# Seven products per tile: ScalarE seeds PSUM banks for TensorE in place of sums on VectorE

## Chip, cores and metric

The kernel runs on one core of one Trainium2 chip. The metric is device time in microseconds; three runs of the kernel before gave 684.82, 685.51 and 687.89, median 685.51.

## The reference

A mixer block and a feed-forward block, each between a layer norm and a residual, on x of 4 x 512 x 512 in fp32, H = 2048:

```python
i, f, g = x @ Wi.T, x @ Wf.T, x @ Wg.T      # x layer-normed
gate = sigmoid(f); v = silu(i) * (1 - gate)
o = scan(gate, v)                            # along the 512 rows
o = rmsnorm(o) * gnorm_w * silu(g) @ Wo.T
x = x + layernorm(o)
h = silu(z @ W1.T) * (z @ W3.T)              # z = layernorm(x), 2048 wide
out = x + layernorm(fwht(h) @ W2.T)          # fwht: Walsh-Hadamard, folded into W2
```

## The kernel before

Each fp32 product is made of three fp16 passes (high x high, high x low, low x high, lines 611 to 613, `three_passes`), each a matmul with 128 rows of weights; weights and inputs are split into a high and a low half beforehand. The four batches b = 0 to 3 go through the same steps, overlapped. Every engine (PE is TensorE, ACT ScalarE, DVE VectorE, POOL GpSimd, SP the queue of the transfers) works through its own table of steps written out by hand at the top of the file (`PE_ORDER`, `ACT_ORDER`, ...), strictly in that order, and the engines meet through semaphores only. A step is named kind.b.index, on PE with the PSUM bank behind the colon. PE's kinds:

- XT: transposes of x; AN, GC, WS, W2S: norms of the weights; F, I, G: the three projections, each 12 matmuls of 512 columns; MS: mean square of o; Y: product with Wo; H2: Hadamard of W2.
- GA, UP (batch 0 only): product of z with a 128-wide chunk of W1 and W3.
- GP, GQ, GR, GU (batches 1 to 3, 16 groups g each): the same for two chunks at once by Strassen-Winograd's seven products. Group g = 2j is W1 for the pair of chunks 2j and 2j+1, g = 2j+1 is W3. A product is 2 x 3 matmuls of 256 columns. GP is P1 (line 796), GQ is P2 and P6 (805), GR P7 and P5 (808), GU P4 and P3 (811), through `two_products` (787); each kind has a bank of its own, and none waits for the result of another, only for its bank to be free and for the loaded weights (`ld_wc`).
- D: product of 128 rows of a hidden chunk with W2, 3 matmuls of 512 columns, 64 per batch, summed in banks 0 to 3; D.b.at is chunk at // 4.

The sums of the seven products are made outside PE. ScalarE's step GP copies P1 to SBUF (`copy_product`, line 986). VectorE's `combine_u2` (line 1282) adds it to P2 and to P6, 512 columns in one add; `combine_u3` (1292, 1295) adds U2 to P7 and P5 and makes one more sum of 256; `combine_last` (1303) adds P4 and P3. ScalarE's GA (line 1007) applies SiLU, VectorE's UP (1346) multiplies by the W3 part, ScalarE's UP (1019) makes the high half and POOL's UP (1434) the low half, after which D may read the chunk. ScalarE's UP also waits for `d_mm`, the D steps that still read its buffer.

PE's wait for a bank is derived from the table: a step waits for whoever read the bank's last contents (`wait_bank`). In VectorE's MS (line 1162) the mean square is read from its bank. The transfers that matter are `load_combined` (line 578, weights of a pair j, three slots), which waits for the products of the pair three back.

Of the kernel before, what the change touches and what calls it, by code (L numbers as in the profile page):

```python
# [1477 lines left out]
```

## Time and profile before

| | |
|---|---|
| median of three runs | 685.51 us (684.82 to 687.89) |
| profiled execution, span of its instructions | 683.7 us |
| PE, PE weight loads | 665.8, 403.8 us busy |
| DVE, ACT, POOL | 479.8, 292.7, 261.6 us busy |
| HBM | 81.92 MB read, 23.07 MB written |

The profile gives the profiled execution by its span, from first to last instruction; what lies around the instructions is in the device time and not in the span. Busy times say how long an engine worked; the idle time of an engine matters only where another one waits for it.

### The profile page before, as it was taken

What the parts mean: (1) busy time and instruction counts of PE and PEld (TensorE: products, weight loads), DVE (VectorE), ACT (ScalarE), POOL (GpSimd) and SP (SyncE); (2) the same over time, 40 slices, a digit from 0 to 9 for tenths busy, and PEclk for the clock granted to TensorE, in tenths of its full rate; (3) what the DMA queues carried; (4) which work ended last, traced back from release to release, by engine and by line L of the source; (5) the groups of instructions that cost most, each with busy time, mean ns of one, the idle gap of its engine ahead of it and who ended that gap; (6) DMA issues with size and microseconds to landing.
All of it is one profiled execution on the core that took longest, in us unless ns stands there. A gap on an engine that the chain in (4) does not pass through costs nothing.

```text
span 683.7 us, 10835 instructions
## 1 busy us (share of the span) xinstructions
PE 665.8 (97%) x4068; PEld 403.8 (59%) x4068; DVE 479.8 (70%) x836; ACT 292.7 (43%) x482; POOL 261.6 (38%) x228
## 2 busy tenths in 40 slices
PE   3999999999999999999999999999999999999996
PEld 2344454444444454567777785657567777777762
DVE  6998889988999878857577463456576555752554
ACT  4898974675245217623232312344234222321231
POOL 1189689558356200534422300233346211111231
PEclk9999999999999999999999999999999999999999
DMA  8961311413789985638496362202526846144122
GB/s 334 393 246 70 135 47 47 139 61 109 236 325 257 233 252 195 227 147 283 143 253 237 108 169 108 108 32 93 199 95 186 184 170 220 36 157 173 57 72 92
DMA packets 58819, 113.29 MB, mean 166 GB/s; under 512 B 33424, under 2 KB 37776, under 8 KB 54160
## 3 DMA queue, kind: packets, MB, share of 16 engines
q1 hardware_dynamic: 58768, 112.61, 49.7%
q8 instruction: 32, 0.52, 0.3%
q14 instruction: 19, 0.16, 0.1%
HBM read 81.92 MB, written 23.07 MB: 154 GB/s over the span
## 4 chain that ended last, share of the span: by engine, by line
PE 93%; DMA 3%; POOL 1%; SPq 1%; DVE 1%; issue 0%; ACT 0%; POOLq 0%; DVEq 0%
PE ps L611 30%; PE ps L613 30%; PE ps L612 30%; PE ps L759 2%; DMA w2t<-W2t 2%; DMA ring<-L_attn_Wf 1%; SPq L518 1%; PE ps L661 1%; POOL w2t L1420 1%; PE ps L720 0%; POOL rstd L1377 0%; POOL x1r L1420 0%; SPq L483 0%; ACT ot L861 0%; PE ps L683 0%
## 5 line engine op out<-in xcount | busy, mean ns | idle before, releaser
L611 PE MATMUL ps<-xb,ring 128*128 128x256 f16 (+1 forms) x704 | 226.0, 321 | 0.4 <-DVE ring L1105 0.4
L613 PE MATMUL ps<-xb,ring 128*128 128x256 f16 (+1 forms) x704 | 225.9, 321 | 0.0
L612 PE MATMUL ps<-xb,ring 128*128 128x256 f16 (+1 forms) x704 | 225.9, 321 | 0.0
L612 PEld LDWEIGHTS ps<-xb,ring 128*128 128x128 f16 x704 | 68.9, 98 | 48.1 <-issue 2.9
L611 PEld LDWEIGHTS ps<-xb,ring 128*128 128x128 f16 x704 | 69.1, 98 | 47.8 <-issue 2.6
L1377 POOL TENSOR_TENSOR rstd<-var,neg_half 128x1 f32<-128x1 f32 x64 | 45.3, 712 | 128.5 <-DVE var L1355 42.6
L613 PEld LDWEIGHTS ps<-xb,ring 128*128 128x128 f16 x704 | 68.9, 98 | 42.1
L1434 POOL TENSOR_TENSOR ring<-sga,ring 128x512 f16<-128x512 f32 x36 | 44.1, 1231 | 106.7 <-ACT ring L1019 106.7
L611 PE MATMUL ps<-ring 128*128 128x256 f16 x288 | 78.5, 273 | 0.0
L613 PE MATMUL ps<-ring 128*128 128x256 f16 x288 | 78.5, 273 | 0.0
L612 PE MATMUL ps<-ring 128*128 128x256 f16 x288 | 78.5, 273 | 0.0
L1434 POOL TENSOR_TENSOR hsp<-sga,hsp 128x512 f16<-128x512 f32 x24 | 28.3, 1190 | 96.6 <-ACT hsp L1019 96.6
L1282 DVE TENSOR_TENSOR ring<-ps,junk 128x512 f32<-128x512 f32 x48 | 33.0, 688 | 41.8 <-PE ps L613 28.5
L1292 DVE TENSOR_TENSOR ring<-ps,ring 128x512 f32<-128x512 f32 x48 | 33.0, 687 | 37.2 <-PE ps L613 36.3
L986 ACT ACTIVATE junk<-ps 128x256 f32<-128x256 f32 x48 | 18.2, 379 | 88.0 <-PE ps L613 84.9
L1303 DVE TENSOR_TENSOR ring<-ps,ring 128x512 f32<-128x512 f32 x48 | 33.0, 687 | 30.9 <-PE ps L613 30.6
L611 PE MATMUL ps<-w2t,ring 128*128 128x512 f16 x144 | 54.6, 379 | 0.0
L612 PE MATMUL ps<-w2t,ring 128*128 128x512 f16 x144 | 54.6, 379 | 0.0
L613 PE MATMUL ps<-w2t,ring 128*128 128x512 f16 x144 | 54.6, 379 | 0.0
L1346 DVE SCALAR_TENSOR_TENSOR sga<-ring,up_c,sga 128x512 f32<-128x512 f32 x48 | 37.1, 784 | 17.1 <-ACT sga L1007 16.1
L1007 ACT ACTIVATE sga<-ring,gate_c 128x512 f32<-128x512 f32 x48 | 34.0, 717 | 34.7 <-POOL hsp L1434 12.1
L1019 ACT ACTIVATE ring<-sga 128x512 f16<-128x512 f32 x36 | 22.2, 624 | 43.4 <-DVE sga L1346 28.2
(174 smaller groups left out, 1193.6 us busy)
## 6 DMA issues: line engine op xcount, KB each, us to landing
ring<-w_comb SPq DMA_DIRECT2D x24, 1792.0 KB, 7.6
ring<-W13t SPq DMA_DIRECT2D x16, 512.0 KB, 7.3
ring<-W13t SPq DMA_DIRECT2D x8, 1024.0 KB, 6.1
w_comb<-ring SPq DMA_DIRECT2D x8, 1024.0 KB, 8.1
rows<-L_attn_hidden_states SPq DMA_DIRECT2D x16, 256.0 KB, 4.6
w2t<-W2t SPq DMA_DIRECT2D x8, 512.0 KB, 10.2
res<-L_attn_hidden_states SPq DMA_DIRECT2D x16, 256.0 KB, 4.5
w_comb<-ring SPq DMA_DIRECT2D x8, 512.0 KB, 2.7
```

The lines of the kernel that those rows point to most:

```text
L611: pe.matmul(dst, a_hi, b_hi, start=start, stop=False)
L612: pe.matmul(dst, a_hi, b_lo, start=False, stop=False)
L613: return pe.matmul(dst, a_lo, b_hi, start=False, stop=stop)
L986: act.activation(p_copy[:, g % 2], bank("GP", b, g)[:, 256:512], ACT.Copy).then_inc(sp_rdy, 1)
L1007: act.activation(sga[:, c % 2], src, ACT.Silu, scale=gate_c[:]).then_inc(sga_rdy, 1)
L1019: act.activation(hid(b, c, 0), sga[:, c % 2], ACT.Copy).then_inc(hid_hi, 1)
L1282: dve.tensor_tensor(combined(g % 2)[:, 0:512].rearrange("p (o t) -> p o t", o=2), bank("GQ", b, g)[:].rearrange("p (o t) -> p o t", o=2), ...
L1292: dve.tensor_tensor(to[:, 512:1024].rearrange("p (o t) -> p o t", o=2), bank("GR", b, g)[:].rearrange("p (o t) -> p o t", o=2), both, ALU. ...
L1303: dve.tensor_tensor(to[:, 512:1024], bank("GU", b, g)[:], to[:, 512:1024], ALU.add).then_inc(gu_rdy, 1)
L1346: dve.scalar_tensor_tensor(sga[:, c % 2], src, up_c[:], sga[:, c % 2], ALU.mult, ALU.mult).then_inc(hid_rdy, 1)
L1377: pool.tensor_tensor(dst, src, neg_half[:].broadcast_to(src.shape), ALU.pow).then_inc(done, 1)
L1434: pool.tensor_tensor(hid(b, c, 1), sga[:, c % 2], hid(b, c, 0), ALU.subtract).then_inc(hid_lo, 1)
```

## The change

The seven products are ordered so that PE does part of the sums itself: a matmul series that doesn't start a bank anew adds to what is in it. GP now makes P1 and P5 in one bank. ScalarE copies P1 into both halves of the GQ bank (`seed_p1`) and P5 to SBUF. PE adds P2 and P6 onto the seed, which gives C11 and U2. ScalarE copies U2 over P1 (`seed_u2`). GR adds P7 onto U2 in the GQ bank and P3 onto the copy of U2 in the GP bank. VectorE adds P5 to each (`sum_c22`, `sum_c12`, 256 columns each), and GU adds P4 onto the half of the GQ bank that `sum_c22` has read. The GQ bank then holds two of the four quarters, which GA and UP for odd chunks read directly; even chunks read the sums in SBUF. GR and GU have no banks of their own. Three VectorE steps per group become two, one ScalarE step becomes two with three copies. All five order tables are new, in the part before the products too: POOL takes X1.1.2 and X1.1.3 ahead of the first butterflies FW, and PE takes F.0.0 ahead of AN.2.

```diff
@@ PE_ORDER (and the tables of ACT, DVE, POOL and SP, all written anew)
-GP.3.6:7 GQ.3.4:5 GR.3.4:6 D.3.0 GQ.3.5:4 GR.3.5:5 D.3.1 GP.3.7:7 GQ.3.6:6 D.3.2 GU.3.4:4 D.3.3
+D.2.63 GQ.3.4:4 D.3.0 GR.3.4 GQ.3.5:5 GP.3.6:7 GU.3.4 D.3.1 GR.3.5 D.3.2 D.3.3 D.3.4 D.3.5 D.3.6 GQ.3.6:4 GP.3.7:6
...
-        p_copy = junk[:].bitcast(F32).rearrange("p (w t) -> p w t", w=2)
-        def combined(w):
-            return kb(46 + 4 * w, 4).bitcast(F32)
+        p5 = junk[:].bitcast(F32).rearrange("p (w t) -> p w t", w=2)
+        def summed(g):
+            return kb(46 + 2 * (g % 4), 2).bitcast(F32)
...
-            at = c % 2 * 2 + t // 2
-            return hid(b, c - c % 2 + (0, 1, 1, 0)[at], part)[:, chunk((0, 2, 0, 2)[at] + t % 2)]
+            return hid(b, c - c % 2 + 1 - t // 2, part)[:, chunk(2 * (c % 2) + t % 2)]
...
+            elif k == "GP":
+                engine.wait_ge(c12_rdy, HC * (n - 1) + u + 1)
+            elif k == "GQ":
+                engine.wait_ge(hid_rdy if u % 2 else sga_rdy, HC * n + 2 * (u // 2) + 2)
...
-            def products_p1(b, g):
+            def products_p1_p5(b, g):
...
+                wait_bank("GP", b, g)
+                dst = bank("GP", b, g)
+                product(dst[:, 0:256], b, g, 0, 0, True, False, False)
+                product(dst[:, 256:512], b, g, 3, 3, False, True, False).then_inc(gp_mm, 1)
             def products_p2_p6(b, g):
-                two_products("GQ", b, g, (1, 1), (4, 4), gq_mm)
-            def products_p7_p5(b, g):
-                two_products("GR", b, g, (5, 5), (3, 3), gr_mm)
-            def products_p4_p3(b, g):
-                wait = up_mm if g % 2 else ga_mm
-                two_products("GU", b, g, (2, 6), (6, 2), wait, 2)
+                n = HC * (b - 1) + g
+                pe.wait_ge(seed_rdy, n + 1)
+                dst = bank("GQ", b, g)
+                product(dst[:, 0:256], b, g, 1, 1)
+                product(dst[:, 256:512], b, g, 4, 4).then_inc(gq_mm, 1)
+            def products_p7_p3(b, g):
+                n = HC * (b - 1) + g
+                pe.wait_ge(u2_rdy, n + 1)
+                product(bank("GQ", b, g)[:, 256:512], b, g, 5, 5).then_inc(gr_mm, 1)
+                pe.wait_ge(p5_rdy, n + 1)
+                product(bank("GP", b, g)[:, 0:256], b, g, 6, 2).then_inc(gr_mm, 1)
+            def product_p4(b, g):
+                n = HC * (b - 1) + g
+                pe.wait_ge(c22_rdy, n + 1)
+                product(bank("GQ", b, g)[:, 256:512], b, g, 2, 6).then_inc(up_mm if g % 2 else ga_mm, 2)
...
-            def copy_product(b, g):
+            def seed_p1(b, g):
                 n = HC * (b - 1) + g
                 act.wait_ge(gp_mm, n + 1)
+                wait_for_bank(act, "GQ", b, g)
+                src = bank("GP", b, g)
+                both = src[:, 0:256].rearrange("p (o t) -> p o t", o=1).broadcast_to((P, 2, 256))
+                act.activation(bank("GQ", b, g)[:].rearrange("p (o t) -> p o t", o=2), both, ACT.Copy).then_inc(seed_rdy, 1)
                 if n > 1:
-                    act.wait_ge(gq_rdy, n - 1)
-                act.activation(p_copy[:, g % 2], bank("GP", b, g)[:, 256:512], ACT.Copy).then_inc(sp_rdy, 1)
+                    act.wait_ge(c12_rdy, n - 1)
+                act.activation(p5[:, g % 2], src[:, 256:512], ACT.Copy).then_inc(p5_rdy, 1)
+            def seed_u2(b, g):
+                n = HC * (b - 1) + g
+                act.wait_ge(gq_mm, n + 1)
+                act.wait_ge(p5_rdy, n + 1)
+                act.activation(bank("GP", b, g)[:, 0:256], bank("GQ", b, g)[:, 256:512], ACT.Copy).then_inc(u2_rdy, 1)
...
-            def combine_u2(b, g):
-            def combine_u3(b, g):
-            def combine_last(b, g):
+            def sum_c22(b, g):
...
+                dve.wait_ge(p5_rdy, n + 1)
+                dve.wait_ge(gr_mm, 2 * n + 1)
...
+                dve.tensor_tensor(summed(g)[:, 256:512], bank("GQ", b, g)[:, 256:512], p5[:, g % 2], ALU.add).then_inc(c22_rdy, 1)
+            def sum_c12(b, g):
...
+                dve.wait_ge(gr_mm, 2 * n + 2)
+                dve.tensor_tensor(summed(g)[:, 0:256], bank("GP", b, g)[:, 0:256], p5[:, g % 2], ALU.add).then_inc(c12_rdy, 1)
```

How the tables move work, at three places. The first is PE in batch 3 at the end of GQ.3.7 (ps5 and ps6 are PSUM banks, `seed`, `u2`, `p5` and `c22` the semaphores of the steps named above; L643 to L645 are the three passes). Before, GR.3.7 follows GQ.3.7 directly in a bank of its own:

```order
L613 MATMUL ps5<-ring 128x256
L611 MATMUL ps4<-ring 128x256 [waits gu_rdy]
L612 MATMUL ps4<-ring 128x256
L613 MATMUL ps4<-ring 128x256
L611 MATMUL ps4<-ring 128x256
L612 MATMUL ps4<-ring 128x256
L613 MATMUL ps4<-ring 128x256
L611 MATMUL ps4<-xb,ring 128x256
```

And with the change, one step D stands between GQ.3.7 and GR.3.7:

```order
L645 MATMUL ps5<-ring 128x256
L643 MATMUL ps0<-w2t,ring 128x512 [waits hid_lo,hid_hi]
L644 MATMUL ps0<-w2t,ring 128x512
L645 MATMUL ps0<-w2t,ring 128x512
L643 MATMUL ps5<-ring 128x256 [waits u2_rdy]
L644 MATMUL ps5<-ring 128x256
L645 MATMUL ps5<-ring 128x256
L643 MATMUL ps5<-ring 128x256
L644 MATMUL ps5<-ring 128x256
L645 MATMUL ps5<-ring 128x256
L643 MATMUL ps6<-xb,ring 128x256 [waits p5_rdy]
```

GR now works in GQ's bank and waits for ScalarE's copy of U2, with D.3.12 in between; the wait before was for the bank alone.

The second is ScalarE in batch 1, between the hidden copies of chunks 10 and 12 (L1019, now L1029) and the products. Before:

```order
L1019 ACTIVATE ring<-sga 128x512 [waits d_mm,hid_rdy] x2
L986 ACTIVATE junk<-ps 128x256 [waits gq_rdy,gp_mm]
L1007 ACTIVATE sga<-ring,gate_c 128x512 [waits hid_lo,gr_rdy]
L1007 ACTIVATE sga<-ring,gate_c 128x512 [waits hid_lo,gu_rdy]
L1019 ACTIVATE hsp<-sga 128x512 [waits d_mm,hid_rdy]
L847 ACTIVATE o_s<-rows 128x512 [waits ld_zt,x_norm]
L1019 ACTIVATE hsp<-sga 128x512 [waits d_mm,hid_rdy]
L1007 ACTIVATE sga<-ring,gate_c 128x512 [waits hid_lo,gr_rdy]
```

With the change, UP.1.10 and UP.1.11 in the first row, then GA.1.12, GA.1.13, GP.1.14 (two copies), UP.1.12, UP.1.13 and GQ.1.14, the seed of U2, and GA.1.14:

```order
L1029 ACTIVATE ring<-sga 128x512 [waits d_mm,hid_rdy] x2
L1017 ACTIVATE sga<-ring,gate_c 128x512 [waits hid_lo,c12_rdy]
L1017 ACTIVATE sga<-ps,gate_c 128x512 [waits hid_lo,ga_mm]
L982 ACTIVATE ps<-ps 128x512 [waits sga_rdy,gp_mm]
L985 ACTIVATE junk<-ps 128x256 [waits c12_rdy]
L1029 ACTIVATE hsp<-sga 128x512 [waits d_mm,hid_rdy] x2
L991 ACTIVATE ps<-ps 128x256 [waits p5_rdy,gq_mm]
L1017 ACTIVATE sga<-ring,gate_c 128x512 [waits hid_lo,c12_rdy]
```

A seed that PE waits for (L991) stands right behind two hidden copies that wait for D; on PE the order there is D.1.39, GQ.1.14, D.1.40, GR.1.14.

The third is PE in batch 3 at MS.3.0, the mean square, followed by Y.3.0. Before, in banks 7 and 4:

```order
L613 MATMUL ps6<-xb,ring 128x256
L720 MATMUL ps7<-ones,osum 128x1 [waits oadd,gr_rdy]
L720 MATMUL ps7<-ones,osum 128x1 x3
L611 MATMUL ps4<-ring,ot 128x512 [waits gu_rdy,o_lo,o_hi]
L612 MATMUL ps4<-ring,ot 128x512
```

With the change both are in bank 6:

```order
L645 MATMUL ps5<-ring 128x256
L711 MATMUL ps6<-ones,osum 128x1 [waits oadd,c12_rdy]
L711 MATMUL ps6<-ones,osum 128x1 x3
L643 MATMUL ps6<-ring,ot 128x512 [waits e_rdy,o_lo,o_hi]
L644 MATMUL ps6<-ring,ot 128x512
```

Y.3.0 now waits for `e_rdy`, VectorE's read of the mean square.

## Rows read from the trace of the kernel before

**Rows 1.** Page: span, busy times, slices of PE and its granted clock
```profile
span 683.7 us, 10835 instructions
...
PE 665.8 (97%) x4068; PEld 403.8 (59%) x4068; DVE 479.8 (70%) x836; ACT 292.7 (43%) x482; POOL 261.6 (38%) x228
...
PE   3999999999999999999999999999999999999996
...
PEclk9999999999999999999999999999999999999999
```

**Rows 2.** Waits of PE, longest group: us, times, longest
```profile
PE ps L661 <- DVE rows L1075: 9.2, 3, 8.4
```

**Rows 3.** Chain that ended last, last matmul: start, us
```profile
672.55 0.23 PE ps L613
```

**Rows 4.** Timeline at 426.7 us: start, us, engine, line, operation
```profile
426.72 0.27 PE L613 MATMUL ps<-xb,ring 128*128 128x256 f16 x1
...
426.83 0.38 PE L611 MATMUL ps<-w2t,ring 128*128 128x512 f16 x1
...
427.03 0.39 ACT L986 ACTIVATE junk<-ps 128x256 f32<-128x256 f32 x1
...
427.05 0.38 PE L612 MATMUL ps<-w2t,ring 128*128 128x512 f16 x1
```

**Rows 5.** Groups by line and shape; the last row is line 850 alone
```profile
L612 PE MATMUL ps<-xb,ring 128*128 128x256 f16 x384 | 104.7, 273 | 0.0
...
L611 PE MATMUL ps<-ring 128*128 128x256 f16 x288 | 78.5, 273 | 0.0
...
L1434 POOL TENSOR_TENSOR ring<-sga,ring 128x512 f16<-128x512 f32 x36 | 44.1, 1231 | 106.7 <-ACT ring L1019 106.7
...
L1346 DVE SCALAR_TENSOR_TENSOR sga<-ring,up_c,sga 128x512 f32<-128x512 f32 x48 | 37.1, 784 | 17.1 <-ACT sga L1007 16.1
...
L1282 DVE TENSOR_TENSOR ring<-ps,junk 128x512 f32<-128x512 f32 x48 | 33.0, 688 | 41.8 <-PE ps L613 28.5 <-issue 6.5 <-ACT sga L1007 3.8
...
L1292 DVE TENSOR_TENSOR ring<-ps,ring 128x512 f32<-128x512 f32 x48 | 33.0, 687 | 37.2 <-PE ps L613 36.3
...
L1303 DVE TENSOR_TENSOR ring<-ps,ring 128x512 f32<-128x512 f32 x48 | 33.0, 687 | 30.9 <-PE ps L613 30.6
...
L1019 ACT ACTIVATE ring<-sga 128x512 f16<-128x512 f32 x36 | 22.2, 624 | 43.4 <-DVE sga L1346 28.2 <-PE ps L613 15.2
...
L1295 DVE TENSOR_TENSOR ring<-ps,ring 128x256 f32<-128x256 f32 x48 | 20.4, 424 | 1.6
...
L986 ACT ACTIVATE junk<-ps 128x256 f32<-128x256 f32 x48 | 18.2, 379 | 88.0 <-PE ps L613 84.9 <-DVE ring L1282 3.1
...
L850 ACT ACTIVATE xb<-ps x8: 572/584/598, 11.9 to 44.0; 128x512 f16<-128x512 f32 x8
```

**Rows 6.** Timeline: an engine's end and the weight load that waited for it
```profile
10.07 1.91 ACT L861 ACTIVATE ot<-ring 128x2048 bf16<-128x2048 f32 x1 [7.84 <-DMA ring<-L_attn_Wf]
...
12.03 0.13 PEld L683 LDWEIGHTS ps<-ot,ones 128*128 128x128 bf16 x2 [2.10 <-ACT ot L861]
...
24.27 1.41 DVE L1105 SCALAR_TENSOR_TENSOR ring<-ring,row_s 128x512 f16<-128x512 f32 x2
...
25.14 0.10 PEld L611 LDWEIGHTS ps<-xb,ring 128*128 128x128 f16 x1 [0.43 <-issue]
```

**Rows 7.** Timeline of PE: AN.2 and the first matmul of F.0.0
```profile
18.98 1.89 PE L683 MATMUL ps<-sga,ones 128*128 128x512 bf16 x4 [0.17 <-ACT sga L861]
...
20.66 0.42 PE L611 MATMUL ps<-xb,ring 128*128 128x512 f16 x1
```

**Rows 8.** Timeline: first matmul of Y.3.0, and VectorE's read for MS.3.0
```profile
484.24 0.38 PE L611 MATMUL ps<-ring,ot 128*128 128x512 f16 x1
...
484.41 0.16 DVE L1162 TENSOR_SCALAR ms_eps<-ps 128x4 f32<-128x4 f32 x1 [2.06 <-PE ps L720]
```

**Rows 9.** Page, DMA issues: count, KB each, us to landing
```profile
ring<-w_comb SPq DMA_DIRECT2D x24, 1792.0 KB, 7.6
```

More of the change, by code:

```diff
@@ L609, in _, with three_passes @@
         def _(pe):
[L610 to L613 removed]
+            def three_passes(dst, a_hi, a_lo, b_hi, b_lo, start, stop, onto=False):
+                pe.matmul(dst, a_hi, b_hi, start=start, stop=False, skip_group_check=onto)
+                pe.matmul(dst, a_hi, b_lo, start=False, stop=False, skip_group_check=onto)
+                return pe.matmul(dst, a_lo, b_hi, start=False, stop=stop, skip_group_check=onto)
@@ L659, in transpose_tile @@
+                wait_for_bank(pe, kind, b, t)
             def transpose_tile(dst, tile):
@@ L778, in up, with product @@
                 hidden("UP", b, c, 1, up_mm)
-            def product(dst, b, j, w, block, q, start, stop):
+            def product(dst, b, g, block, q, start=False, stop=True, onto=True):
+                j, w = divmod(g, 2)
                 for k in range(2):
@@ L783, in product @@
                     b_hi, b_lo = comb_z(b, q, 0)[:, k, :], comb_z(b, q, 1)[:, k, :]
-                    last = three_passes(dst, a_hi, a_lo, b_hi, b_lo, start and k == 0, stop and k == 1)
+                    last = three_passes(dst, a_hi, a_lo, b_hi, b_lo, start and k == 0, stop and k == 1, onto)
                 return last
-            def two_products(kind, b, g, one, two, done, by=1):
-                j, w = divmod(g, 2)
-                n = HC // 2 * (b - 1) + j
-                wait_bank(kind, b, g)
-                dst = bank(kind, b, g)
-                if one:
-                    product(dst[:, 0:256], b, j, w, *one, True, False)
-                product(dst[:, 256:512], b, j, w, *two, not one, True).then_inc(done, by)
-            def products_p1(b, g):
+            def products_p1_p5(b, g):
                 j, w = divmod(g, 2)
@@ L999, in ga @@
                 else:
-                    act.wait_ge(gu_rdy if c % 2 else gr_rdy, n - HC + 1 - c % 2)
-                    src = combined(0)[:, c % 2 * 512:c % 2 * 512 + 512]
+                    g = 2 * (c // 2)
+                    if c % 2:
+                        act.wait_ge(ga_mm, n + 1)
+                        src = bank("GQ", b, g)[:]
+                    else:
+                        act.wait_ge(c12_rdy, HC * (b - 1) + g + 1)
+                        src = summed(g)
                 if n == 0:
@@ L1343, in up @@
                 else:
-                    dve.wait_ge(gu_rdy if c % 2 else gr_rdy, n - HC + 2 - c % 2)
-                    src = combined(1)[:, c % 2 * 512:c % 2 * 512 + 512]
+                    g = 2 * (c // 2) + 1
+                    if c % 2:
+                        dve.wait_ge(up_mm, n + 1)
+                        src = bank("GQ", b, g)[:]
+                    else:
+                        dve.wait_ge(c12_rdy, HC * (b - 1) + g + 1)
+                        src = summed(g)
                 dve.scalar_tensor_tensor(sga[:, c % 2], src, up_c[:], sga[:, c % 2],
```

365 lines of the change are left out of this document (164 added, 201 removed).

## Prediction

> **What bounds the kernel now.** The page first: TensorE (PE) is busy for 665.8 of 683.7 us at the full granted clock, VectorE (DVE) for 70%, ScalarE (ACT) for 43%; of the 40 slices only the first and the last are below 9 [rows 1]. The waits of PE come next: the longest group is 9.2 us, 8.4 of it the start of the program, and the five groups together make 12.2 us, all before 25.2 us [rows 2]. From then to the last matmul at 672.55 us [rows 3] PE waits for nobody. That its busy time is real shows in the starts of single matmuls: 256 columns take 0.11 us to the next start, 512 take 0.22 [rows 4]. So the 647 us between are PE's own work, and a change can move the end in three ways only: change that work, change the 25 us ahead or the 11 us behind, or make PE wait where it doesn't today.
>
> **The work of PE.** Per product group (b, g) there are 7 products of 6 matmuls of 256 columns before and after; only their grouping changes, from 1+2+2+2 to 2+2+2+1. The trace has 3 x (384 + 288) = 2016 such matmuls [rows 5], which is 48 groups x 42. Cost: 0.
>
> **VectorE and ScalarE.** Removed per group on VectorE: 688 + 687 + 424 + 687 = 2486 ns; added: two adds of 256 columns, 2 x 424 = 848 ns [rows 5]. Over 48 groups VectorE loses 79 us of work (479.8 to about 401). ScalarE had one copy of 379 ns; it gets a seed of 512 columns, a copy of 256 to SBUF and a seed of 256. No row shows ScalarE writing PSUM; the nearest are its copies out of PSUM, 584 ns for 512 columns and 379 for 256 [rows 5]. I take these, so 1.34 in place of 0.38 us, +46 us in all (292.7 to about 339). Bounds: from 0.1 us less to 0.1 us more for each. Neither total is worth anything in itself, since PE waits for neither engine [rows 2]; both stay under 60%.
>
> **What is new: PE waits inside a group.** Before, no product needed another engine's answer; ScalarE and VectorE only had to free a bank. Now a group is a relay: P1, P5 on PE; seed on ScalarE; P2, P6; seed of U2 on ScalarE; P7, then P3; sum on VectorE; P4. One round trip costs: last matmul start to the start of the engine that waits, 0.31 us (426.72 to 427.03) [rows 4]; the operation; and the hand-over to PE, which is 0.05 us from ScalarE (10.07 + 1.91 to 12.03) and about 0.15 from VectorE (the first of two splits in the 1.41 us from 24.27, so an end near 25.0, to 25.14); I use 0.05 to 0.19 [rows 6]. What PE is given to do meanwhile I count from the two order tables: one step D is 3 x 0.216 = 0.65 us, one product of six 0.65; counted from the last matmul's start that is 0.65 + 0.11 = 0.76 us.
>
> - Seed of U2, the first place shown above: in 10 of 48 groups exactly one step of 0.65 us stands between (3.7, 2.6, 1.15 and so on). Needed: 0.31 + 0.38 + (0.05 to 0.19) = 0.74 to 0.88, there are 0.76. Wait 0 to 0.12, taken 0.06: 10 x 0.06 = 0.6 us. The other 38 have 1.3 us and more: 0.
> - Sum ahead of P4: in 10 groups only P3 stands between. Needed: 0.31 + 0.42 + (0.05 to 0.19) = 0.78 to 0.92 against 0.76. Wait 0.02 to 0.16, taken 0.09: 0.9 us.
> - First seed: one group (1.4) has one step, 0.76 us against 0.31 + 0.58 + (0.05 to 0.19) = 0.94 to 1.08: 0.3 us. The 47 others have at least 1.3 + 0.11: 0.
> - Step MS.3.0 and Y.3.0 now share bank 6, and Y.3.0 waits for VectorE's read. In the trace Y's first matmul starts at 484.24 and that read ends at 484.41 + 0.16 [rows 8]; with the hand-over 484.62 to 484.76: 0.4 us.
>
> On a round trip 0.1 us weighs 2 us over the twenty tight ones, so where the seed is written matters. The rows have PSUM to SBUF only. The Trainium skill (Perfetto Trace Analysis, Optimizing Scalar/DVE Operations) puts ScalarE's access overhead at about 93 ns on SBUF and 51 on PSUM; by that each U2 seed would be some 0.04 us shorter and the first term 0.2 in place of 0.6 us, an estimate from that page that no run here shows.
>
> **Queues.** ScalarE works in order, so a step that waits holds the seeds behind it. The tightest such place is the second shown above. UP.1.12 waits for the end of D.1.39 (its buffer is read until then). Call the issue end of D.1.39 zero: ScalarE starts at 0.2, two hidden copies of 0.626 take it to 1.45; GQ.1.14 ends on PE at 1.30, so its seed can start at 1.50 and is done at 1.88; PE wants GR.1.14 at 1.30 + 0.65 = 1.95. It fits, with 0.02 to spare after a hand-over of 0.05. Five more places (GP.2.2, GR.2.0, GQ.1.13, GQ.3.10, GQ.3.11) come out between 0.1 short and 0.3 spare; I take 0.2 us for all. The hidden values reach D later relative to it: least distance from the last product of a pair to the step D that reads it was 7.8 us, is now 4.55 (D.2.40), against 0.31 + 0.78 + 0.63 + 1.23 + hand-overs of 0.3 = 3.25 us [rows 5]; the sum of 0.69 that stood in it is gone. Cost 0, spare 1.3 us, or some 0.6 with one SiLU of about 0.7 queued ahead. If that cover went, each 0.1 us would show as a wait of D for GpSimd.
>
> **Transfers.** SP's and POOL's queues are reordered too. The weights of a pair are loaded when the pair three back is done; least distance in the order was 13.0 us, is 15.6, for 7.6 us to landing [rows 9]: 0. On POOL the first butterflies of W2 move behind two short powers; the first matmul on them comes after the attention part of batch 0: 0.
>
> **The head.** AN.2 (512 columns, four matmuls, 1.89 us at the pitch of 0.43 that PE shows before 20.66, its 1.2 GHz level) moves behind F.0.0 [rows 7]. F.0.0 may start that much earlier than 20.66. But I.0.0 at 25.17 waits for a VectorE split behind the same six operations as before, so it stays near 25.2 to 25.6, while XT.1.1 (0.43) is already done. Bounds: 0.4 less, or 2.1 more if F.0.0 itself runs at the low clock and so delays AN.2 and that split. Taken: 0. The tail (last statistics, power, output) is the same instructions behind the same order of D: 0.
>
> **Sum.** 0.6 + 0.9 + 0.3 + 0.4 + 0.2 = 2.4 us on a span of 683.7, so 686.1. The median of the runs shown, 685.5, is 1.8 above this span, which is what lies around the program; with it 687.9. Since all hand-overs were taken at mid-range and the order leaves hardly any place without at least one step, I put the point at 687.5. 0.5% of the time is 3.4 us, about what can be told from no change: 682.1 and 688.9 are the borders.
>
> **Rivals.**
> 1. No wait at all: hand-overs at 0.05 and seeds shorter than 0.38 us fit in 0.76. Then only MS.3.0 is left: 685.5 to 686. For it: only steps that fit nearly exactly were put between. Against: the sum ahead of P4 is 0.02 short even so. Chance 0.24.
> 2. Slower: the relay is late throughout. Place: U2 seeds, sums ahead of P4 and the seeds behind a hidden copy on ScalarE. Price: with a hand-over of 0.35 us and a seed of 0.48, needed are 1.14 and 1.08 against 0.76, so 10 x 0.38 + 10 x 0.32 = 7.0 us, 0.7 for the first seed and about 1 in the queues: 694. It decides, against the border of 3.4 us, from 0.14 us a tight round trip on average (0.9 being spent elsewhere). The head's 2.1 us works the same way. Chance 0.25.
> 3. Clock: short repeated waits bring PE to its 1.2 GHz level, where 512 columns take 0.43 in place of 0.22 us; 20 us of that would cost 10: 697. Against it: the waits at 24 to 25 us left the granted clock and the pitch alone [rows 1, 6]. The Trainium skill (TensorE: Matmul & The Clock Gate, A second HAM failure mode) describes a kernel in which small idles between groups made the clock swing; this trace, whose banks turn as fast, does not show it. Chance 0.02.
> 4. Faster by more than 3.4 us: PE would have to lose most of its 12.2 us of early waits, 8.4 of which are the load of x. Chance 0.02.
> My own case, 686 to 688.9, keeps 0.47.
>
> **Numbers.** Faster 0.02 (rival 4); slower 0.26 (rivals 2 and 3, less what of rival 2 ends under the border); within 0.5%: 0.72. The range 684.6 to 692.0 holds my case, rival 1 and the nearer two thirds of rival 2.
>
> **What would show it.** Right: VectorE near 400 us busy, ScalarE near 340; PE waits of 0.02 to 0.2 us, released by the seed of U2 and the sums, 20 to 30 of them, and one of 0.4 at MS.3.0 near 494 us; PE busy and clock unchanged. Wrong: waits over 0.3 us at most tight places, waits of D for GpSimd, a first I.0.0 later than 26 us, or a granted clock under 1 after 25 us.

## The result, and the profile after

The change makes the kernel slower: 709.82 us median of six runs (708.54 to 715.08) against 685.61 (684.82 to 687.89, six runs), ratio 1.0361, 95% interval 1.0326 to 1.0396. The forecast was 687.5 with a range from 684.6 to 692.0. The profiled execution is the longest of the six, 715.08 us with a span of 713.3.

Page of the change, against [rows 1]:

```profile
span 713.3 us, 10836 instructions
...
PE 678.4 (95%) x4068; PEld 404.0 (57%) x4068; DVE 412.7 (58%) x740; ACT 337.9 (47%) x578; POOL 268.0 (38%) x228
...
PE   3899989999989989999999998999999999999996
...
PEclk9899999999999989999999999999999999999999
```

The engines' work is about as forecast: 4068 matmuls as before, ScalarE 338 us, VectorE 413. But four slices of PE between the first two and the last are below 9, and two slices of the granted clock. Before there was none. Groups of the change, against [rows 5]:

```profile
L1291 DVE TENSOR_TENSOR ring<-ps,junk 128x256 f32<-128x256 f32 x48 | 20.3, 422 | 129.5 <-PE ps L645 104.1
...
L982 ACT ACTIVATE ps<-ps 128x512 f32<-128x512 f32 x48 | 27.9, 582 | 32.6 <-PE ps L645 24.2
...
L991 ACT ACTIVATE ps<-ps 128x256 f32<-128x256 f32 x48 | 17.7, 369 | 43.5 <-PE ps L645 43.1
```

The seeds (L982, L991) and sums last what the nearest rows of before had said: 582, 369 and 422 ns against 584, 379 and 424. Waits of PE, against [rows 2] (waited for, us, times, longest):

```profile
PE ps L652 <- DVE rows L1085: 12.1, 5, 8.1
PE ps L643 <- DVE w2t L1321: 3.0, 1, 3.0
PE ps L643 <- ACT ps L982: 3.0, 1, 3.0
PE ps L652 <- DVE rows L1198: 2.6, 1, 2.6
PE ps L643 <- DMA xb<-osq: 2.2, 1, 2.2
PE ps L681 <- DVE osq L1129: 1.6, 1, 1.6
PE ps L643 <- ACT sg L905: 1.3, 1, 1.3
PE ps L750 <- ACT sg L905: 1.1, 1, 1.1
...
PE ps L643 <- DVE ms_eps L1172: 0.3, 1, 0.3
```

These are not many short waits at the relay, but single waits of 1 to 3 us at places the forecast had not looked at: ZT.0.0 at 99.2 us (L1198), GA.0.14 at 209.4 (L1321), GQ.1.0 at 260.7 (L982), F.2.3 at 298.9 (L905), F.3.0 at 439.7 (the transposed rows of x). The largest group is, but for 8.1 us of start, the transposes XT in batches 0 and 1. Of all the waits listed only the one at GQ.1.0 is for a seed.

To follow the loss I matched PE's steps with its records. Start of the first record of a step, us, in the profiled executions:

| | XT.1.3 | ZT.0.0 | UP.0.8 | GA.0.14 | GQ.1.0 | D.3.42 |
|---|---|---|---|---|---|---|
| before | 42.0 | 92.6 | 152.3 | 197.1 | 242.4 | 663.5 |
| the change, this trace | 45.7 | 99.2 | 161.9 | 209.4 | 260.7 | 693.1 |
| the change, second trace (below) | 44.5 | 98.0 | 160.0 | 208.0 | 258.7 | 687.2 |

So 18 of the 29.6 us by which this span is longer, and 16 of 24 in the second trace, are lost ahead of the first seed or on it. The rest falls between there and 440 us but for some 3 (1.6 in the second trace).

### The profile page after: what moved, and what is told of

It is laid out like the page before. It is cut to its first block, busy times and chain, and to the rows that moved or that the text cites. A ratio compares the mean times of both kernels' runs of the same rounds, so it can differ in the third digit from the quotient of the medians.

```text
span 713.3 us, 10836 instructions
## 1 busy us (share of the span) xinstructions
PE 678.4 (95%) x4068; PEld 404.0 (57%) x4068; DVE 412.7 (58%) x740; ACT 337.9 (47%) x578; POOL 268.0 (38%) x228
## 4 chain that ended last, share of the span: by engine, by line
PE 62%; DVE 10%; DMA 7%; issue 4%; SPq 2%; POOL 2%; DVEq 2%; ACT 1%; POOLq 0%; ACTq 0%
PE ps L643 20%; PE ps L645 20%; PE ps L644 20%; DMA ring<-W13t 6%; DVEq L1073 2%; DVE ring L1278 1%; SPq L556 1%; PE ps L750 1%; DVE ring L1267 1%; DVE ring L1269 1%; DVE st L1072 1%; DMA xb<-osq 1%; DVE ring L1271 1%; POOL res L1430 1%; POOL rstd L1377 1%
## 5 line engine op out<-in xcount | busy, mean ns | idle before, releaser
L643 PE MATMUL ps<-xb,ring 128*128 128x256 f16 (+1 forms) x704 | 229.4, 326 | 10.8 <-DVE w2t L1321 3.0
L644 PE MATMUL ps<-xb,ring 128*128 128x256 f16 (+1 forms) x704 | 229.3, 326 | 0.0
L645 PE MATMUL ps<-xb,ring 128*128 128x256 f16 (+1 forms) x704 | 229.1, 325 | 0.0
L643 PEld LDWEIGHTS ps<-xb,ring 128*128 128x128 f16 x704 | 69.8, 99 | 65.4 <-issue 7.9
L644 PEld LDWEIGHTS ps<-xb,ring 128*128 128x128 f16 x704 | 69.6, 99 | 48.9 <-issue 4.8
L1291 DVE TENSOR_TENSOR ring<-ps,junk 128x256 f32<-128x256 f32 x48 | 20.3, 422 | 129.5 <-PE ps L645 104.1
L645 PEld LDWEIGHTS ps<-xb,ring 128*128 128x128 f16 x704 | 69.7, 99 | 44.0 <-issue 2.8
L1434 POOL TENSOR_TENSOR ring<-sga,ring 128x512 f16<-128x512 f32 x36 | 48.1, 1343 | 107.2 <-ACT ring L1029 107.2
L643 PE MATMUL ps<-ring 128*128 128x256 f16 x288 | 78.9, 274 | 0.0
L645 PE MATMUL ps<-ring 128*128 128x256 f16 x288 | 78.8, 274 | 0.0
L643 PE MATMUL ps<-w2t,ring 128*128 128x512 f16 x144 | 54.8, 381 | 0.0
L644 PE MATMUL ps<-w2t,ring 128*128 128x512 f16 x144 | 54.8, 381 | 0.0
L645 PE MATMUL ps<-w2t,ring 128*128 128x512 f16 x144 | 54.8, 381 | 0.0
L1017 ACT ACTIVATE sga<-ps,gate_c 128x512 f32<-128x512 f32 x40 | 27.3, 683 | 33.8 <-PE ps L645 28.9
L982 ACT ACTIVATE ps<-ps 128x512 f32<-128x512 f32 x48 | 27.9, 582 | 32.6 <-PE ps L645 24.2
L1346 DVE SCALAR_TENSOR_TENSOR sga<-ps,up_c,sga 128x512 f32<-128x512 f32 x40 | 29.8, 746 | 18.8 <-PE ps L645 16.4
L1029 ACT ACTIVATE ring<-sga 128x512 f16<-128x512 f32 x36 | 22.1, 624 | 37.7 <-DVE sga L1346 23.3
L1395 POOL TENSOR_TENSOR ot<-sg,ot 128x512 f16<-128x512 f32 x16 | 23.1, 1445 | 43.4 <-ACT ot L915 43.3
L991 ACT ACTIVATE ps<-ps 128x256 f32<-128x256 f32 x48 | 17.7, 369 | 43.5 <-PE ps L645 43.1
```

Source lines behind the costliest of these rows:

```text
L643: pe.matmul(dst, a_hi, b_hi, start=start, stop=False, skip_group_check=onto)
L644: pe.matmul(dst, a_hi, b_lo, start=False, stop=False, skip_group_check=onto)
L645: return pe.matmul(dst, a_lo, b_hi, start=False, stop=stop, skip_group_check=onto)
L982: act.activation(bank("GQ", b, g)[:].rearrange("p (o t) -> p o t", o=2), both, ACT.Copy).then_inc(seed_rdy, 1)
L991: act.activation(bank("GP", b, g)[:, 0:256], bank("GQ", b, g)[:, 256:512], ACT.Copy).then_inc(u2_rdy, 1)
L1017: act.activation(sga[:, c % 2], src, ACT.Silu, scale=gate_c[:]).then_inc(sga_rdy, 1)
```

## Experiments

Each time is a median of four runs, beside six or seven of the kernel before on the same chip (medians 685.2 to 686.2). An expectation gives a theory and a rival, each with its range. Of the theories' ranges only those of e2, e4 and, in its traced execution, e18b held; e1 ended 0.6 us and e8 1.9 us below its range, the others above theirs.

### First part or seeds

**e1 and e2** exchange the first part of all five tables (PE up to D.0.50, about 240 us), where the two kernels have the same steps in another order.

```diff
 PE_ORDER = """
-XT.0.0:0 XT.0.1:1 XT.0.2:2 XT.0.3:3 AN.0.0:4 AN.1.0:5 GC.0.0:6 F.0.0:7 AN.2.0:0 AN.3.0:1 XT.1.0:4 XT.1.1:2 I.0.0:6
+XT.0.0:4 XT.0.1:5 AN.0.0:6 XT.0.2:7 XT.0.3:0 GC.0.0:1 AN.1.0:2 AN.2.0:3 F.0.0:4 XT.1.0:5 AN.3.0:6 I.0.0:7
...
```

> The changed kernel (seeds by ScalarE, batches 1 to 3) with the first part of all five order tables taken from the kernel before: batch 0 and the start of batch 1, about the first 240 us, in which neither kernel has a seven-product group. Theory A (the rewritten order of batch 0 costs 11 to 15 us of the 24): 695 to 699 us, and TensorE's record up to 240 us like that of the kernel before, with F.0.0 at 20.7 us and no wait of over 1.5 us before 240. Rival B (the seeds cost it all, wherever a seven-product group stands): no change, 707 to 712 us.

> The mirror image: the kernel before, with its sums on VectorE in batches 1 to 3, and only the first part of the five tables (up to about 240 us) taken from the change. Theory A: 697 to 701 us. Rival B: 685 to 687 us, as before. If the two halves add up, (e2 - before) + (e1 - before) = after - before = 24 us.

e1: 694.41 us, ratio 1.0138 (1.0113 to 1.0163). e2: 697.41, 1.0176 (1.0152 to 1.0200). e2 has no seed at all and carries 11.9 us of the loss. e1, with all seeds, carries 8.9. Together 20.8 of 24.2; the 3.4 left come on top where both meet. Rival B, that the seeds cost it all, is out. e2 loses its time ahead of 240 us and nothing behind: GQ.1.0 starts at 254.8, D.3.42 at 675.9, 421.1 us apart as before.

**e6** takes the tables of before only up to about 155 us.

> The changed kernel with the order tables of before up to about 155 us (TensorE up to UP.0.8, ScalarE to WT.15.1, VectorE to P.1.3, GpSimd to P.1.3), and the change's own order from there on. By the lags that I read from the trace of the change: 10 us are lost ahead of 155 us, 4.7 between 155 and 240 (all behind H2.6 and H2.7 at 209). Theory A (the places cost each by itself): 699 to 702 us. Rival B (the loss at 209 us is a consequence of the late batch 0, and vanishes with it): 694 to 697 us, as with the longer stretch of before.

706.05 us, 1.0297 (1.0278 to 1.0316): 4 us less than the change, not 8 to 11. PE reaches UP.0.8 at 152.4 us as before, but GA.0.14 only at 202.1 and GQ.1.0 at 254.0. So the stretch from 155 to 240 us costs by itself (rival B of this run is out). It is dearer here than in the change: UP.0.8 to GQ.1.0 takes 101.7 us, 98.9 and 98.7 in the two traces of the change and 90.1 before. 1.4 of it is a new wait ahead of GA.0.9 at 156.5 us, the first step behind the seam between the two tables, which no trace of either kernel has. And of the 7.6 us by which UP.0.8 is earlier than in the second trace of the change, 4.6 are left at GQ.1.0.

### Is it the seeds

**e10 and e11** are e1's kernel without the second seed and without both; **e12** is the whole change without both. The sums in these kernels lack U2, or P1 and U2, so they don't compute the block; all products and the copy of P5 stay. The edit of e11 and e12, in part (e10 has only the last line and drops the second copy):

```diff
-                pe.wait_ge(seed_rdy, n + 1)
+                wait_bank("GQ", b, g)
                 dst = bank("GQ", b, g)
-                product(dst[:, 0:256], b, g, 1, 1)
-                product(dst[:, 256:512], b, g, 4, 4).then_inc(gq_mm, 1)
+                product(dst[:, 0:256], b, g, 1, 1, True, False, False)
+                product(dst[:, 256:512], b, g, 4, 4, False, True, False).then_inc(gq_mm, 1)
...
-                pe.wait_ge(u2_rdy, n + 1)
```

> The kernel with seeds and the first 240 us of before, without ScalarE's second copy: U2 is left out of C12, and TensorE goes from P6 to P7 without a wait; 48 copies of 0.37 us less on ScalarE. Theory A (this handover costs some 1 to 2 us in 48 groups): 692.5 to 694 us against 694.4. Rival (it costs 0.1 us and more in every group): 686 to 690 us.

> The same without both seeds: P1 is left out of the bank of P2 and P6 too (each sum lacks its seeds), TensorE waits for the bank alone, and ScalarE keeps the P5 copy only, 45 us less work. Theory A: the wait for the weight sums' chain at 247 us (2.4 us) and the handovers go, the banks' places and F.3.0 stay: 689 to 691.5 us. Rival (all that is left behind 240 us is the relay): 685.5 to 687.5 us.

> The whole change with its own order tables, but without both seeds (each sum lacks P1 and U2), so that no product waits for ScalarE's copies. Theory A (the order costs most of the 24 us, the handovers and the seed at 260 us 5 to 9): 700 to 705 us. Rival B (the handovers are the cost): 686 to 692 us.

e10: 694.17 us (1.0097 to 1.0171). e11: 693.86 (1.0102 to 1.0155). e12: 712.98 (1.0374 to 1.0456). All against 694.4 and 709.8 with seeds: taking them out gains nothing that can be measured, in either kernel. All three end above my ranges, e10 by 0.2 us, e11 by 2.4, e12 by 8. Waits of PE in e12:

```profile
PE ps L643 <- ACT sga L1010: 3.9, 1, 3.9
PE ps L643 <- DVE w2t L1314: 3.2, 1, 3.2
PE ps L652 <- DVE rows L1191: 2.6, 1, 2.6
```

(The line numbers of this kernel are up to 7 lower.) The second and third stand where they stood. The 3.0 us ahead of GQ.1.0 are gone, and 3.9 stand ahead of I.2.0, 18 us later, whose bank is freed by the same queue of ScalarE.

**e3** moves the step that holds the first seed up.

```diff
-ZT.1.6 SH.4.0 XT.2.0 XT.2.1 XT.2.2 XT.2.3 SH.5.0 GP.1.0 GQ.1.0 GP.1.1 GA.1.0 SH.6.0 W.0.0 GA.1.1 W.0.1 F.2.0 W.0.2
+ZT.1.6 SH.4.0 XT.2.0 XT.2.1 XT.2.2 XT.2.3 GP.1.0 GQ.1.0 SH.5.0 GP.1.1 GA.1.0 SH.6.0 W.0.0 GA.1.1 W.0.1 F.2.0 W.0.2
```

> The changed kernel with one step moved on ScalarE: SH.5.0 (waits for VectorE's weight sums, which wait for a DMA) stands behind GP.1.0 and GQ.1.0 instead of ahead of them, as it stood behind GP.1.0 before. Theory A (the 3.1 us wait ahead of GQ.1.0 at 260 us is this queue, and the half-speed stretch behind it, 1.5 to 3 us, is its consequence): 703.5 to 706.5 us, 3 to 6 us less than the change, and no slice of low clock at 260 us. Rival (SH.5.0 is late for something else, or the wait only moves to the next step): 708 to 711 us.

714.85 us, 1.0418 (1.0388 to 1.0448): no gain, and above the rival's range too. The wait is gone from GQ.1.0 and is at I.2.0, longer, for GA.1.0, which now is behind SH.5.0:

```profile
PE ps L643 <- ACT sga L1017: 4.8, 1, 4.8
```

**e4** makes the second handover longer: four copies of 64 columns, 213 ns each, 0.85 us for 0.37.

> The changed kernel with ScalarE's second copy (256 columns, 0.37 us) issued as four of 64 columns, some 0.9 us together by its fixed part: the relay's second handover is 0.5 us later in each of 48 groups. Theory A (the relay waits little, since other products stand between; it is hidden except at the few places where no product of the down projection stands between): 1 to 7 us more, 711 to 716 us. Rival B (the relay is late nearly everywhere, and its lateness is what the change costs): 48 times 0.5 = 24 us more, 730 to 735 us.

715.18 us, 1.0432 (1.0415 to 1.0449), 5.4 above the change's median, where 48 x 0.48 = 23 us were put in. Most of the relay is covered. In the trace PE's listed waits for the copies are two, 1.1 us together, so they don't make up the 5.4; the rest stays open, with the change's own runs 9 us apart.

### Which wait ahead of 240 us

**e5, e13, e17b, e14** each move one to three steps out of the way of a late one, and **e15** has the edits of e5, e13 and e14 together.

```diff
 e5:  -F.0.0:7 AN.2.0:0                       +AN.2.0:0 F.0.0:7
 e13: -P.1.0 FD.2.0 MS.0.0 FD.2.1             +FD.2.0 MS.0.0 FD.2.1 P.1.0
 e14: -FD.7.4 FD.7.5 UP.0.12 FD.7.6 SO.1.0    +SO.1.0 FD.7.4 FD.7.5 UP.0.12 FD.7.6
      -UP.0.11 GA.0.12 YN.1.0 SH.1.0          +SH.1.0 UP.0.11 GA.0.12 YN.1.0
 e17b:-WQ.2.0 WQ.3.0 P.0.2 WN.7.0 G.0.3 S.0.3 I.1.0 P.0.3
      +P.0.2 G.0.3 S.0.3 I.1.0 P.0.3 WQ.2.0 WQ.3.0 WN.7.0
```

> The changed kernel with two neighbours on TensorE changed back: AN.2.0 (four 128x512 products, for which VectorE waits 2.1 us) ahead of F.0.0, as before. Theory A (F.0.0 starts 1.2 us earlier than before, but all of it runs at a pitch of 0.43 us, 1.2 GHz, and pushes AN.2.0, and with it the weights of the next products, to 24.5 us): I.0.0 starts 1.5 to 2.5 us earlier than 28.4, and the time falls by 1 to 2.5 us, to 707 to 709. Rival (the head is late for the transposes XT.0.1 to XT.0.3 and the loads, whatever stands there): no change, 709 to 711.

> The change with one step moved on VectorE: P.1.0 three steps later (behind FD.2.0, MS.0.0, FD.2.1). In the change VectorE stands 3.0 us idle at 72.8 us in front of P.1.0, for ScalarE's G.1.0, in the stretch in which it is 85 to 95% busy. Theory C (the loss at ZT.0.0, 99 us, is VectorE's queue, and everything behind it hangs on the chain of the weight sums, whose first load starts at the end of UP.0.8): ZT.0.0's wait of 2.6 us shrinks to under 1, UP.0.8 and the first load come 2 to 4 us earlier, and the time falls by 2 to 5 us, to 705 to 708. Rival D (the 3 us are filled by something else, as when AN.2.0 was put back): no change, 709 to 712.

> The whole change, with its own tables, and three small moves: AN.2.0 ahead of F.0.0 on TensorE, P.1.0 three steps later on VectorE, SO.1.0 and SH.1.0 earlier. Theory C: the three together bring back 6 to 11 us of the 24, 699 to 704 us. Rival D: 707 to 711 us.

> The change with ScalarE's squares WQ.2.0, WQ.3.0 and WN.7.0 (5.0 us) moved from ahead of G.0.3 to behind P.0.3. The last try aimed at the wrong step: VectorE's 3.0 idle us at 72.8 stand ahead of P.0.3, not P.1.0, and end with ScalarE's G.0.3, which stands behind these squares (G.0.3 ran at 72.1 us in the change, at 60.2 before). Theory C (VectorE, 85 to 98% busy from 50 to 155 us, bounds batch 0, and idle time there is not made up): no idle stretch over 1 us ahead of P.0.3, ZT.0.0 waits under 1 us instead of 2.6, the first load of the weight sums comes 2 to 4 us earlier, and the time is 705 to 708.5 us. Rival D (its queue is filled by other waits): 709 to 715 us.

> The kernel with the tables of before up to 155 us (706.05) with one round of the weight sums put earlier in the queues: SO.1.0 ahead of FD.7.4, FD.7.5 and UP.0.12 on VectorE, SH.1.0 ahead of UP.0.11 on ScalarE. Theory C (load, sums, SH, SO of each round run one behind the other; a round that is 5 us late moves all that follow, and the waits ahead of GA.0.14, 3 us, and GQ.1.0, 3.6 us, with their stretches at half clock): SA.2.0 starts at 193 to 194 us instead of 197.1, GA.0.14 waits under 1.5 us, and the time is 700 to 703.5 us. Rival D (each round is held up by something of its own): 705 to 707 us.

| | median us | interval of the ratio | XT.1.3 | ZT.0.0 | UP.0.8 | GA.0.14 | GQ.1.0 |
|---|---|---|---|---|---|---|---|
| e5 | 711.78 | 1.0351 to 1.0406 | 43.0 | 98.3 | 161.0 | 208.8 | 262.0 |
| e13 | 712.48 | 1.0339 to 1.0434 | 43.0 | 95.9 | 157.9 | 205.5 | 256.7 |
| e15 | 713.89 | 1.0398 to 1.0429 | 43.9 | 99.2 | 162.4 | 212.9 | 262.6 |
| e17b | 713.10 | 1.0383 to 1.0434 | 42.4 | 98.5 | 160.5 | 208.5 | 261.8 |
| e14 (on e6) | 706.36 | 1.0288 to 1.0325 | 42.0 | 92.5 | 152.2 | 204.3 | 254.7 |

None gains in its median. The starts are of one execution each, and small differences among them say little: before and e1, with the same tables there, reach XT.1.3 at 42.0 and 43.6 us. e13's is its fastest, 707.66; it is 2 us ahead of the change's second trace from ZT.0.0 to GQ.1.0, though VectorE still stands idle for 3.5 us ahead of P.0.3, and its three other runs took 711.9 to 715.9. e5 shows how a wait comes back. The head is 2.7 us earlier than in the first trace of the change and 1.5 than in the second (XT.1.3), and the wait at ZT.0.0 grows from 2.6 in both to

```profile
98.32 1.16 PE L652 MATMUL ps<-ident,rows 128*128 128x128 f32 x8 [4.07 <-DVE rows L1198]
```

e17b shows why. In the change VectorE stands idle for ScalarE's G.0.3 (L905), which is behind squares of the weights (L946, L952) in ScalarE's queue; timeline of the change:

```profile
69.86 1.06 ACT L946 ACTIVATE junk<-ring 128x1024 bf16<-128x1024 f32 x1 [0.15 <-DMA ring<-W13t]
...
72.09 0.67 ACT L905 ACTIVATE sg<-ps,unscale 128x512 f32<-128x512 f32 x1
...
72.79 1.15 DVE L1168 SCALAR_TENSOR_TENSOR sg<-sg,g_coef,o_s 128x512 f32<-128x512 f32 x1 [3.04 <-ACT sg L905]
```

(e13 had taken the waiting step for P.1.0; it is P.0.3.) With the squares behind it G.0.3 runs at 66.3 us. But ScalarE now stands idle for 2.15 us ahead of it, for GpSimd's P.0.2 (L1395), the squares end later, and PE waits for them at WS.0.0, which sums them. Waits of e17b:

```profile
PE ps L736 <- ACT junk L946: 2.9, 1, 2.9
```

ScalarE is busy for 19.5 and 19.4 of the 20 us from 60 to 80, before and in the change, and VectorE for 54.8 of the 56 from 99 to 155 (51.7 before). In a queue that full a step moved forward pushes another back, or meets an input that is not there yet. In e14 VectorE stopped 2.8 us for a result of GpSimd in front of the step moved, and PE for 3.4 us at H2.7.0.

### The part behind 240 us

**e7, e9, e16** begin from e1 and mend what is late behind it.

```diff
 e16: -GP.1.0:6 D.0.51 D.0.52 GQ.1.0:5 D.0.53 GP.1.1:7
      +GP.1.0:6 D.0.51 D.0.52 D.0.53 D.0.54 D.0.55 D.0.56 D.0.57 GQ.1.0:5 D.0.58 GP.1.1:7
      -D.1.52 F.3.0:6 D.1.53 D.1.54 D.1.55 I.3.0:6
      +D.1.52 D.1.53 D.1.54 F.3.0:6 D.1.55 D.1.56 I.3.0:6
 e7:  and group 1 behind the attention:
      +G.2.2:6 I.2.3:7 G.2.3:5 GQ.1.1:6 GP.1.2:7 GR.1.1 GU.1.1 MS.2.0:4
```

> The kernel with seeds and the first 240 us of before, and three places mended behind them: GQ.1.0 five steps of the down projection later, so that the weight sums' chain (SA.5.0, SH.5.0) is over before TensorE needs the seed; group 1 of batch 1 behind the attention of batch 2, so that F, I and G go over three banks again, as before; F.3.0 two steps later behind its transposes. Theory A (what is left of the loss at 247 to 284 and 423 us is places, not seeds): 687.5 to 690.5 us. Rival (the seeds need what stands there, and the waits only move): 693 to 696 us.

> The kernel with seeds and the first 240 us of before, with the transition from batch 1's first group over the attention of batch 2 to its Y products put as in the kernel before, on all engines: GQ.1.0 seven steps of the down projection later, GP.1.1 inside the attention, no product of groups 2 and 3 ahead of Y.2.3 (so that the weights from DRAM, for which the first mending waited 2.1 us, have time), F, I, G over three banks, F.3.0 two steps later. Theory A (what is left between 247 and 305 us is places): 688.5 to 691 us, no wait over 1 us between 240 and 430. Rival (a seed needs a bank for longer than a sum does, so that the four banks are short wherever the products stand): 694 to 697, with waits for ACT sga, ACT ps or DVE ring at new places.

> The kernel with seeds and the first 240 us of before (694.4), with two of the first mending's three parts: GQ.1.0 five down steps later, and F.3.0 two steps later; group 1 stays where the change has it. Theory C (those two waits are the queue of the weight sums and the transposes, and GP.1.2's wait in the first mending was the third part's): 690.5 to 692.5 us. Rival D (TensorE's later start only meets the next wait, at I.2.0 and at G.2.0): 693.5 to 695.5 us.

e7: 696.03 us (1.0125 to 1.0161). e9: 700.95 (1.0193 to 1.0253). e16: 693.18 (1.0089 to 1.0123), the lowest with seeds but only 1.2 below e1, and the two intervals overlap; still slower than before. e9 is slower than e1 and than its rival's range. In e7 the wait of 2.3 us ahead of GQ.1.0 is gone and new ones took its place, one ahead of GP.1.2 for weights that are summed and stored in this very stretch:

```profile
PE ps L643 <- DMA ring<-w_comb: 2.1, 1, 2.1
PE ps L643 <- ACT sga L1017: 1.6, 1, 1.6
```

In e9 they run up to 3.0 us, from the attention of batch 2 to GP.1.3. I found no order by hand that keeps all queues fed.

### Waits and the clock

**e18b** is the change once more, **e8** the kernel before with three waits put in.

```diff
+                if (b, at - 1) in STALLS:
+                    pe.wait_ge(st_end, STALLS[b, at - 1])
...
+            def stall(n, k):
+                pool.wait_ge(st_go, n + 1)
...
+                for i in range(k):
...
+                    pool.tensor_tensor(osum[:], osum[:], osum[:], ALU.add).then_inc(st_end, 1)
```

> The change itself once more, for a second trace of it. Its six runs lay between 708.5 and 715.1 us, the mean granted clock of those listed between 0.981 (715.1) and 0.999 (708.5). Theory: an execution at 0.99 and more shows the same waits at the same places (99, 209, 260, 299, 440 us), but matmuls at a pitch of 0.216 us behind most of them, and lies at 708.5 to 711 us; one at 0.98 to 0.985 shows 0.43 us behind them and lies at 712 to 716 us. Rival: the waits themselves differ between executions by as much.

> The kernel before, with three waits put on TensorE in quiet places (behind D.2.45, D.3.5 and D.3.24): GpSimd starts on the product's end and runs 1, 3 and 2 additions of 128x512 (1.3 to 1.5 us each) before TensorE may go on: some 1.7, 4.3 and 3.0 us, 9 together. Theory A (after a wait of over some 1.3 us TensorE runs at half its clock, and so loses another 1 to 3 us): 697 to 701 us, with a pitch of 0.43 us behind the two longer waits. Rival (the low clock in the change has another cause, and a wait costs its own length): 694 to 695 us, with a pitch of 0.216 us behind all three.

The change again: 708.63 us (706.34 to 715.35), 1.0346 (1.0292 to 1.0400); mean granted clocks 0.998, 0.995, 0.996 and 0.983 for 706.3, 708.1, 709.2 and 715.4 us. The waits stand at the same places and differ by up to 0.4 us in length; one of 0.7 us ahead of D.0.0 at 217.5 is new, where the first trace had lost the time to the clock at GA.0.14. What differs more is the clock behind them. GQ.1.0 in the first trace and in the second, by windows (us, PE busy, PEclk):

```profile
260.00:262.00 2.00, 1.27 (x7) 0.50 0.64 120
262.00:264.00 2.00, 2.00 (x9) 0.50 0.78 311
264.00:266.00 2.00, 2.00 (x9) 0.50 0.98 297
266.00:268.00 2.00, 2.00 (x14) 0.82 0.98 381
```

```profile
258.00:260.00 2.00, 1.35 (x13) 1.00 0.59 111
260.00:262.00 2.00, 2.00 (x18) 1.00 0.78 319
262.00:264.00 2.00, 2.00 (x17) 1.00 1.00 317
```

After 2.97 us of waiting, PE ran for six more us at 1.2 GHz, with half as many matmuls; after 2.56 us in the other execution none. At GA.0.14 it was half after 3.0 us and full after 3.3. The fastest run of the change, 706.3, is 20.5 us above the kernel before beside it: that much is there each time. The slowest is 9 us above the fastest and has the lowest clock; for the two traced executions, 5.9 us apart, the windows show it. That all of the spread is the clock is not shown: e4 took 715.4 us at 0.997.

e8: 695.11 us (692.80 to 696.13), 1.0130 (1.0107 to 1.0153). The three waits of the profiled execution, and PE's pitch behind the longest:

```profile
PE ps L613 <- POOL osum L1450: 7.2, 3, 3.7
```

```profile
603.15 0.39 PE L613 MATMUL ps<-w2t,hsp 128*128 128x512 f16 x1 [3.74 <-POOL osum L1450]
603.38 0.38 PE L614 MATMUL ps<-w2t,hsp 128*128 128x512 f16 x1
603.60 0.38 PE L615 MATMUL ps<-w2t,hsp 128*128 128x512 f16 x1
```

They are shorter than planned, the pitch behind is 0.22 us, and this execution took 692.8 us at a clock of 0.999, 6.6 above before. The three others had 0.991 to 0.995 and took 694.8 to 696.1. So here the waits cost their own length, and 3.7 us left the clock at full. That the three others lost the rest to the clock behind a wait is read from their mean clocks alone; no trace shows them. The rival was nearer, though 0.1 us under the median: that is 9 us up, for 7.2 of waits.

## Why the prediction was wrong

**What held.** PE's work (term 0): 4068 matmuls, 256 columns at 0.11 us. The durations of seeds and sums. ScalarE 337.9 us for 339; VectorE 412.7 for 401, its weight splits and butterflies being slower in the new order (the splits of 512 columns, L1261, 1152 ns for 1101 before, the butterflies' two forms, L1316, 944 and 911 for 744 and 786), in e1 404.6. The prediction's 672.55 us is the last matmul of the chain that it shows; PE's own last starts at 677.57. The sum doesn't use it.

**The relay, forecast 2.4 us.** From the distances between neighbouring steps of PE from 305 to 680 us in the trace of the change:
- Seeds of U2, forecast 0.6: no distance over the plain pitch; e10 agrees. The copy fits in one step D. Written to PSUM it took 369 ns against 379 to SBUF, so 0.01 us less and not the 0.04 of the prediction's estimate.
- Sums ahead of P4, forecast 0.9: 9 of the 10 places forecast, 0.08 to 0.10 each, 0.79. One of them, last matmul of P3 and first of P4, 0.19 in place of 0.11:

```profile
590.63 0.42 DVE L1291 TENSOR_TENSOR ring<-ps,junk 128x256 f32<-128x256 f32 x1 [4.47 <-PE ps L645]
590.81 0.27 PE L644 MATMUL ps<-xb,ring 128*128 128x256 f16 x1
590.92 0.27 PE L645 MATMUL ps<-xb,ring 128*128 128x256 f16 x1
...
591.11 0.28 PE L643 MATMUL ps<-ring 128*128 128x256 f16 x1
```

- MS.3.0 and Y.3.0, forecast 0.4: 0.48 (start to start 0.59, before 0.11).
- First seeds, forecast 0.3, and queues, 0.2: 0.62 ahead of GQ.1.4, GQ.1.5 and GQ.1.6.
- Not in the forecast: GP directly behind GU, which waits for the bank that `sum_c12` frees, 5 places, 0.74 together, and 0.39 ahead of GP.1.8 and GP.2.8.

That is 3.0 us in place of 2.4, inside my case, but the nearness is in part luck: 0.6 of the sum did not come, and 1.1 came that it had no term for. Rival 2, the relay late throughout, did not come; its 8.7 us of price are not to be had where both seeds are gone and the time stays (e11, e12).

**The step that failed: the head and the transfers, taken at 0, and the queues, at 0.2 us, as the whole price of the new order outside the groups.** I had noted that all five tables were new in the part before the products too, and then priced that part by one exchange, AN.2 against F.0.0, and by two reordered queues. PE had no wait from 25.2 us on before, and I took "the same steps in another order" for "no wait" without following the queues of ScalarE and VectorE through batch 0, which are nearly as full as PE's. e2 prices it at 11.9 us. Behind 240 us I looked for tight places inside the groups and not where the groups meet other work: the seed GP.1.0 behind SH.5.0, the attention of batch 2 over two banks in place of three (F.2.3 waits 1.3 us for bank 6), F.3.0 for its transposes. The expected profile had named the sign: a first I.0.0 later than 26 us (28.4), waits over 0.3 us, a clock under 1 after 25 us.

**The head's bound.** F.0.0 running at the low clock was named as a bound of 2.1 us and taken at 0. It came: in the change its twelve matmuls go at 0.43 us from 19.48 on, by windows (us, PE busy, PEclk):

```profile
20.00:22.00 2.00, 2.00 (x7) 0.50 1.03 405
22.00:24.00 2.00, 2.00 (x6) 0.50 1.02 408
24.00:26.00 2.00, 2.00 (x12) 0.90 1.04 414
```

In e13 and e17b, with the same order on PE, they went at 0.22. But most of what e5 won back there was waited away at ZT.0.0 (98.3 us against 99.2 and 98.0 in the change), so the term was not where the loss is decided.

**Rival 3, the clock, 0.02.** Its half is true: the clock did fall, after single waits of 2.2 to 3.0 us and not after short repeated ones; the 1.3 us ahead of F.2.3 left it alone. That the waits at 24 us before had left it alone was no evidence for longer ones. The Trainium skill (TensorE: Matmul & The Clock Gate, A second HAM failure mode) tells of small idles between groups that make the clock swing; the 19 waits of 0.08 to 0.23 us here did not do it: from 267 us on the clock is below full only from 440.8 to 444.2 us, behind the wait ahead of F.3.0.

**What is shown and what stays open.** Shown: about half of the loss is in the order of the first 240 us, which has no seed in it. Nearly all of the rest is there without seeds too (e11, 8.7 us above before): in the new order behind 240 us and in what the new grouping asks of banks and sums, which no run parts. The seeds' handovers are worth nothing that a run tells. Not shown is a single cause for the 12 us, nor which of the five tables carries it; none was exchanged alone. The moves of one to three steps brought nothing; in e3, e5, e14 and e17b a wait came back at a neighbour. That the serial chain of the weight sums (load, sums, SH, SO) carries the loss from 160 to 260 us is my reading of e3, e6 and e7, and e14, made to test it, did not get that chain earlier (round 2 at 197.4 us, 197.1 in e6). The traces show that the chain is late, by 9.1 us in round 0 (VectorE's first sum at 170.3 us against 161.2) and by 16.2 in round 5 (255.1 against 238.9), and that rounds 0 to 3 wait 0.8 to 2.1 us for their loads, where before none did. Whether PE is late for the chain or the chain for PE they do not tell.

## To carry to other kernels

When a change rewrites an order written out by hand, price the order apart from the idea: exchange the tables where the steps are the same, and run both halves. A kernel whose main engine never waits is no proof of slack in the others; read the fullest window of each helper, and take "same steps, other order" as an unknown with its own range. And before a wait is mended, ask who sets the end of the next one: here three mended waits were found again 8 (e17b), 19 (e3) and 55 us (e5) later.

## What was not expected of the hardware

ScalarE wrote PSUM from PSUM as fast as SBUF from PSUM, 582 against 584 ns for 512 columns and 369 against 379 for 256, and the 512 columns were read by a broadcast of 256, at no extra cost; a copy of 64 columns took 213 ns. The clock behind a wait of some 3 us was at half in one execution and full in another of the same kernel, at the same place.
